# Loads of x and stores of its normalised rows in pieces of 1 KB instead of 10 KB, x on one queue, small fills on POOL's queue

## What is computed

```
x = x + L0_gnn(layernorm(x))     # per relation r (8): sum over edges of w_e * h[src], then block-diagonal W_r
x = x + L0_ffn(layernorm(x))     # 2 of 8 experts, GELU, layer norm at the end
x = x + L1_gnn(layernorm(x))     # attention over edges, 8 heads
x = x + L1_ffn(layernorm(x))     # 8 experts, each three matmuls deep, gated per node
```

## Time and profile before

| | |
|---|---|
| median of 3 runs | 4971.62 us (4966.54 to 4971.88) |
| the profiled execution | 4976.67 us, of which the span is 4974.8 us |
| mean granted TensorE clock | 0.845 |
| busy share of the span | PE 83%, POOL 63%, DVE 40%, ACT 18% |
| DMA | 544.12 MB in 261824 packets, mean 109 GB/s |

### The profile page before, as it was taken

The page is one execution under the profiler, slowest core; times in us unless marked ns, Lnnn a source line. Parts: engine busy times, 40 slices in busy tenths (PEclk is TensorE's granted clock), DMA queues, the critical chain, the costliest instruction groups (busy, mean ns, idle before and its releaser), DMA issues. The chain is left out here.

```text
span 4974.8 us, 68847 instructions
## 1 busy us (share of the span) xinstructions
PE 4129.4 (83%) x18994; PEld 3224.9 (65%) x18994; DVE 2014.2 (40%) x8073; ACT 893.6 (18%) x1881; POOL 3131.4 (63%) x3258
## 2 busy tenths in 40 slices
PE   1777787788778877858887579999999999999998
PEld 1777777777777777746555246666666666666665
DVE  4445555545555455524444223323332333233321
ACT  3011111111111111113332001121111111111112
POOL 0777777777777777720000677777777777777750
PEclk6677777776777777679998789999999999999999
DMA  4344444444444444421111544444444444444430
GB/s 141 107 121 121 122 122 121 121 121 121 121 122 122 121 122 122 121 70 36 41 38 37 151 116 119 122 123 127 117 125 126 122 117 125 127 122 118 126 94 9
DMA packets 261824, 544.12 MB, mean 109 GB/s; under 512 B 64061, under 2 KB 156091, under 8 KB 260395
## 3 DMA queue, kind: packets, MB, share of 16 engines
q0 software_dynamic: 155232, 432.49, 31.6%
q1 hardware_dynamic: 63015, 65.71, 4.2%
q10 hardware_dynamic: 43398, 44.20, 2.7%
HBM read 482.17 MB, written 59.99 MB: 109 GB/s over the span
## 5 line engine op out<-in xcount | busy, mean ns | idle before, releaser
L645 POOL DMA_INDIRECT ring<-xn,index x1612 | 1531.2, 950 | 606.4 <-issue 477.1
L1554 POOL DMA_INDIRECT ring<-table,index x1616 | 1561.0, 966 | 549.1 <-issue 492.4
L760 PE MATMUL bank<-spare,ring 128*128 128x64 f32 x6448 | 1058.0, 336 | 442.0 <-DMA ring<-xn,index 388.7
L760 PEld LDWEIGHTS bank<-spare,ring 128*128 128x128 f32 x6448 | 1021.7, 250 | 468.8 <-issue 386.3
L1725 PE MATMUL bank<-ring,acc 128*128 128x264 f32 x3232 | 879.5, 408 | 138.2 <-DMA ring<-table,index 133.6
L1725 PEld LDWEIGHTS bank<-ring,acc 128*128 128x128 f32 x3232 | 595.2, 194 | 445.1 <-DMA ring<-table,index 262.2
L1903 DVE TENSOR_SCALAR acc<-iota,off 128x128 f32<-128x128 f32 x1734 | 354.0, 294 | 637.8 <-ACT off L1567 634.9
L1741 PE MATMUL bank<-acc,wa 128*128 (+1 forms) x832 | 383.3, 604 | 26.9 <-ACT ework L1602 26.9
L839 DVE TENSOR_SCALAR spare<-iota,scal 128x64 f32<-128x64 f32 x1612 | 403.4, 332 | 0.0
L859 DVE TENSOR_TENSOR cells<-cells,bank 128x128 f32 x812 | 233.5, 288 | 417.8 <-PE bank L760 335.5
L1766 PE MATMUL bank<-wo,ework 128*128 128x256 f32 x1664 | 378.0, 380 | 1.8 <-DVE y L1974 1.8
(11 more groups left out here) (264 smaller groups left out, 3260.0 us busy)
## 6 DMA issues: line engine op xcount, KB each, us to landing
ring<-table,index POOLq DMA_INDIRECT x1616, 2.8
ring<-xn,index POOLq DMA_INDIRECT x1612, 2.8
sums<-acc ACTq DMA_DIRECT2D x101, 132.0 KB
sums<-spare ACTq DMA_DIRECT2D x101, 128.0 KB
acc<-sums ACTq DMA_DIRECT2D x13, 528.0 KB
y<-x SPq DMA_DIRECT2D x13, 512.0 KB
table<-frow SPq DMA_DIRECT2D x48, 132.0 KB
nsums<-sums ACTq DMA_DIRECT2D x49, 128.0 KB
```

Source lines behind the costliest of these rows:

```text
L645: pool.indirect_dma_start(ring[:, m * BT + t, :], None, k.xn_d, bass.IndirectOffsetOnAxis(ap=index[m][:, t:t + 1], axis=0)).then_inc(got[m ...
L760: ins = pe.matmul(win[q][:, t, h * CELLS:(h + 1) * CELLS], ring[:, m * BT + q * QUAD + t, h * P:(h + 1) * P], onehot[:, q * QUAD + t, :], ...
L1554: pool.indirect_dma_start(ring[:, par * BT + t, :], None, k.table1_d, bass.IndirectOffsetOnAxis(ap=index[par][:, t:t + 1], axis=0)).then_i ...
```

## The change

The view `by_parts` is turned: partition p now holds, in place t, row 125t+p. A chunk is then 1250 rows that lie together in DRAM, but each partition's ten rows lie 125 rows apart there, ten pieces of 1 KB. All five loads of x are issued by ACT, first of all. The nine stores of zero rows and the eight loads of relation weights move from SP's queue to POOL's, behind POOL's fills; the two loads of x that POOL issued are gone from it. SP goes from the store of `base_d` straight to the stores of the normalised chunks. The semaphores follow.

```diff
-            return dram.rearrange("(p t) d -> p t d", t=ROWS_X)
+            return dram.rearrange("(t p) d -> p t d", p=PARTS_X)
...
             pool.wait_ge(filled, 6)
-            for c in (1, 3):
-                pool.dma_start(x[:, chunk(c), :], by_parts(g["x"])[:, chunk(c), :]).then_inc(xloads[c], 16)
             pool.iota(due_i[:], [[P, ROUNDS0]], base=FIRST0, channel_multiplier=0).then_inc(filled, 1)
             pool.iota(part_i[:], [[1, 1]], base=0, channel_multiplier=1).then_inc(filled, 1)
             pool.wait_ge(filled, 8)
+            past_waits(pool, k)
+            for r in range(0, AHEAD, P):
+                n = min(P, AHEAD - r)
+                pool.dma_start(k.x2_all[r:r + n, :], zeros[:n, 0:D]).then_inc(k.padded, 16)
+                pool.dma_start(k.sums_d[r:r + n, :], zeros[:n, :]).then_inc(k.padded, 16)
+            pool.dma_start(k.sums0_d[0:AHEAD0, :], zeros[:AHEAD0, 0:D]).then_inc(k.padded, 16)
+            w = g["L0_gnn_weight"].rearrange("r (b i o) -> b i r o", i=32, o=32)
+            for b in range(D // 32):
+                q = 32 * (b % 4)
+                pool.dma_start(k.wblk[q:q + 32, b // 4, :, q:q + 32], w[b]).then_inc(k.wload, 16)
...
             sp.dma_start(k.base_d.rearrange("(q k) -> q k", k=BLOCKS), base_c[:]).then_inc(stored, 16)
-            sp.wait_ge(filled, 6)
...
             for c in range(CHUNKS_X):
                 sp.wait_ge(x_made, c + 1)
                 sp.dma_start(by_parts(k.xn_d)[:, chunk(c), :], x[:, chunk(c), :]).then_inc(x_stored, 16)
             sp.wait_ge(stored, 16)
-            sp.wait_ge(padded, 16 + 32 * -(-AHEAD // P))
+            sp.wait_ge(k.padded, 16 + 32 * -(-AHEAD // P))
...
-            for c in (0, 2, 4):
+            for c in range(CHUNKS_X):
                 act.dma_start(x[:, chunk(c), :], by_parts(g["x"])[:, chunk(c), :]).then_inc(xloads[c], 16)
```

More of the change, by code:

```diff
@@ L261, in edge_tables @@
         w_loaded, flag_step, flag_done = a.sem("w1g_loaded"), a.sem("flag_step"), a.sem("flag_done")
-        padded = a.sem("padded")
         s, based, cast, offset = a.sem("edge_steps"), a.sem("based"), a.sem("cast"), a.sem("offset")
@@ L267, in edge_tables @@
         stored = a.sem("edge_stored")
-        hard = a.sems("x_loaded", 3)
-        xloads = [hard[0], k.xload[0], hard[1], k.xload[1], hard[2]]
+        xloads = a.sems("x_loaded", CHUNKS_X)
         x_steps, x_spread, x_rooted, x_scaled = (a.sem(f"x_{n}") for n in ("steps", "spread", "rooted", "scaled"))
@@ L2140, in build @@
         k.had = [16 * QUAD * (BATCHES // 4 + (t * QUAD < LAST_TILES)) if t < 4 * QUADS else 0 for t in range(2 * BT)]
-        k.wload, k.xload = a.sem("wload0"), a.sems("xload", 2)
+        k.wload, k.padded = a.sem("wload0"), a.sem("padded")
         k.passed = a.sem("passed")
```

## The result

Over 20 runs each the changed kernel takes 4978.01 us (median) and the kernel before 4969.47, a ratio of 1.0018 with a 95% interval of 1.0012 to 1.0025: 8.5 us slower (6 to 12 by the interval). The forecast was slower by 19.5 us. The direction held and the size was too large by a factor of more than two.

The account below looks back on a forecast made before the run. The first gather's start, set by SP's wait for the last stores, moves everything; five engines' terms, 5 + 17 + 56.9 + 6 + 58.8 + 2 = 145.7 us instead of 126.2, gave +19.5 us, 4991. Range 4976 to 5014.

Parts of the forecast that it names:

- What bounds, what carries x: Opening before the first gather: its start moves all that follows; x, in and out, runs on five DMA engines.
- The price of a piece: Loads and stores of x: a 1 KB piece on five engines costs 47 ns, with 38.5 and 59 kept as alternatives.
- I take 47: Loads and stores of x: 47 ns per 1 KB piece, chosen between a store's 47.7 and a long average from 44.0.
- The sum: One of the five engines in the opening: start, edges, x in, others, x out and landing total 145.7 us.
- the store at a third of the share: Earlier trace's store, read as 47.7 ns a piece at 0.350 share; used as the argument against cheaper pieces.
- the rival's guess: Loads and stores of x: five engines may not meet the memory's limit that 16 meet; chance 0.16.
- the rule of the Trainium skill: Loads and stores of x: about 3 extra cycles per packet, giving 42 ns a piece and +7 us.
- ACT's hold: ACT's five issues of x: held until 929 pieces per engine are through, so the cast comes at 70 us, not 57.
- Which of the two ends last: End of the opening: the engines end at 145.7 us, ACT's last store could at 139.4, 6.3 us in hand.
- pieces are cheap: Loads and stores of x: a piece costs 42 ns or less, +7 us, 4979 in all; chance 0.16.
- Edges first: Edge loads at the start: little of x takes turns with them, so they land at 22 us, not 57.
- Parts at nothing: SP losing 17 issues, POOL gaining 17 at 0.64 us each, DVE's waits: all hidden, no effect on the time.

Follow-up runs that it names:

- e4: Changed kernel, but ACT issues only chunk 0 of x and SP the others behind its edge loads: 4979.3 us against 4970.5, ratio 1.0013.
- e3: Changed kernel with only the view turned back to 10 KB pieces: ratio 1.0009 (0.9983 to 1.0035).
- e7: Kernel before with only the zero rows and relation weights moved to POOL's queue: ratio 0.9999 (0.9979 to 1.0019).
- e6: Kernel before with each transfer of x cut into partitions 0 to 111 and 112 to 124: 4961.33 us, ratio 0.9975.
- e5: Changed kernel with each transfer of x cut into partitions 0 to 111 and 112 to 124: 4954.68 us, ratio 0.9963.
- e9: Changed kernel, x cut at partition 112, 1 KB pieces, SP issuing all loads of x behind the edge loads: ratio 0.9965 (0.994 to 0.9989).

## Why the prediction was off in size

- **What bounds, what carries x.** Right: it is the opening that moves, x is on five engines after the change, the three-dimensional view doesn't widen it (five semaphore writes; 29 with the cut).
- **The price of a piece: the step that failed.** "I take 47": it is 42.3 ns. The sum multiplies the error by 2460, 4.7 x 2460 = 11.6 us of the 19.5. With 42.3 its engine bound is 134.1 us, and e4, where nothing else binds, has 132.4. The 47 came from rows with another number of engines at work. The argument against a cheaper piece was the earlier trace rows, "the store at a third of the share". But its 35.0% is the mean of a wait and a burst; the windows view of the same stretch:

```profile
2253.20:2253.70 0.50, 0.50 (x1) 0.01 (x1) 0.50 (x3) 0.00 (x0) 0.00 (x0) 0.50 0.05 16
2253.70:2254.20 0.50, 0.50 (x2) 0.34 (x1) 0.50 (x2) 0.23 (x1) 0.00 (x0) 0.50 1.00 344
```

  At 344 GB/s over all sixteen engines a piece takes 16 x 1024 / 344 = 47.6 ns, and the earlier trace rows is sixteen full engines too (16 x 1 us / 361 = 44.3 ns). Five engines alone, at 121 GB/s, do it in 42.3. So 44 to 48 ns is the price with sixteen engines busy. Why they pay more than five is not shown; the rival's guess was the memory's limit.
- **A second fault, in the formula.** Share x 16 x time / packets assumes that the records of an engine's packets don't overlap. For the 10 KB pieces it holds. In the changed kernel's own stretch it gives 0.340 x 160 us / 1183 = 46.0 ns, 5.4 engines' worth of records on five engines, where packets per engine and time give 42.3. This can have raised the price from the earlier trace rows; in the earlier trace rows and in the burst of the earlier trace rows both ways give the same.
- The estimate by the rule of the Trainium skill (DMA: Bandwidth & Descriptors, "Why small descriptors are slow (HBM only)"), 42 ns and +7 us, was the better one; the trace agrees, 42.3 ns. It stood as a rival because the rows seemed dearer.
- **ACT's hold.** Right in kind, and nearly in size once the price is: 22 + 889 x 0.0423 + 6 = 65.6 us, and ACT is free at 63.65 (its cast, behind the table load, comes at 65.08). The prediction counted 75 pieces per engine that a queue takes ahead. Here it is about 97: in 63.65 to 85 us 1739 packets of ACT's queue are still carried, 348 per engine, of which 251 are the fifth issue's. SP is held in the same way in e4, for 51.42 us; with 10 KB pieces in e3 the five issues take 4.62.
- **Which of the two ends last.** Forecast: the engines, with 6.3 us in hand. Measured: ACT's chain, the engines idle for some 3 us between 95 and 115. The cheaper piece turns the order. It is the rival "pieces are cheap" (ACT free at 65, normalise(4) at 121), whose +7 us missed the backlog of the store before the last: that one, issued at 112.4, takes 250 x 0.0423 = 10.6 us, to 123.0, 2.3 us beyond the end of normalise(4).
- **Edges first.** Forecast 22 us, measured 28.0 in e4, 45.6 with 10 KB pieces in e3, 57.2 before. The turn-taking was right, the time 6 us short, and hidden behind ACT's hold. The sum gave the edges the whole rate of the engines; in 15 to 25 us of e4 POOL's queue, with the zero rows and the weights, has 31% of it.
- **Parts at nothing.** POOL's 17 issues end at 23.1 us, as said. On their own they go with an opening 1.6 us longer (e7), which is within the spread of repeats; in the changed kernel any such delay of the edges is hidden too.
- **The sum in its parts, by gnn0's start:** before 127.3; queues and fills moved, 10 KB pieces: 125.1 (-2.2); 1 KB pieces with ACT free: 133.6 (+8.5, where 2500 x 3.8 ns = 9.5 would be the full price); ACT held: 137.1 (+3.5). Together +9.8 in the trace, +8.5 in the medians. Taken in the other order, the view alone adds 5.5 us and the moves then add 4.3: five issues of small pieces hold ACT longer than three. The steps compare traces from different chips, and repeats of an opening differed by 0.3 to 2.6 us, so the -2.2 is no firmer than "a little less".

## What to carry to other kernels

Ask first how many DMA engines a transfer gets: 125 partitions went on five here. A cut into 112 and 13 alone took 9 us off the kernel before (e6), about as much as the change cost, and 26 us off the changed kernel's opening (e5). A piece's price is to be read as engines x time / packets, in a stretch that is full and on as many engines as will carry it. A share averaged over a stretch may be a burst and a wait: narrow windows tell. A long transfer in small pieces holds the engine that issues it for nearly as long as it runs, so it belongs on a queue with nothing urgent behind it; small pieces on another queue do let larger ones through, which pays only if the engine behind them is free to use it.

## What the runs showed that was not expected

- The records of 1 KB packets on one DMA engine can overlap: the share of five full engines reads 0.34 instead of 0.31, and in e9 the share of all sixteen reads 1.11 in 25 to 35 us, more than there are engines.
- ACT's second issue of x alone lasted 26.8 us and the later ones 10.5 to 10.9 us each (250 pieces of 42.3 ns are 10.6). This fits an issue that returns when the one ahead of it has been taken over by the engines' queues.
- Cutting over 16 engines isn't 3.2 times as fast: e5's store of a chunk moves 1.28 MB in about 4.8 us, some 270 GB/s against 121.
- Among the chips used, the kernel before took 4970 us on some and 6335 to 6343 us on others. The changed kernel's opening is equally long on both (137.1 and 136.5 us). What makes the later stages longer there was not looked into.
